# Decoder layer on one core: projected keys leave PSUM once as f32, and GpSimd makes both of their f16 parts

## What is computed

```python
q = _qdq(x) @ _qdq(wq).T + bq                  # x: the normed output of self-attention
kv = cond @ wkv.T + bkv                        # cond = ctx_2048: (16, 1500, 256) -> 512 columns
k, v = jnp.split(kv, 2, axis=-1)
q, k, v = ...                                  # 16 heads of 16
scores = jnp.einsum('bhnd,bhmd->bhnm', q, k) * Dh ** (-0.5)
out = softmax(scores) @ v
```

## Time and profile before

| what | us |
|---|---|
| median of 3 runs | 855.14 |
| lowest and highest run | 854.62, 862.06 |
| the profiled execution | 854.35 |
| its span, first to last instruction | 852.5 |

### The profile page before, as it was taken

How to read it: one execution, slowest core, us unless ns; L and a number is a source line. 1 busy time by engine, 2 the same in 40 slices (tenths; PEclk the granted TensorE clock), 3 DMA queues, 4 the chain that set the end, 5 groups by cost and what they waited for, 6 DMA issues and landing times.

```text
span 852.5 us, 30042 instructions
## 1 busy us (share of the span) xinstructions
PE 774.4 (91%) x12379; PEld 582.8 (68%) x12379; DVE 638.2 (75%) x1234; ACT 511.5 (60%) x1084; POOL 296.9 (35%) x366
## 2 busy tenths in 40 slices
PE   5689989999998999999999999999898899999996
PEld 3366666576666666666666666666665579999995
DVE  5877777868877878785977778786875745688887
ACT  2347656566565657655665666666665543787772
POOL 3263216223712371254126421732270003143232
PEclk9899999999999999999999999999999899999999
DMA  7356554554645546554655655565467976766643
GB/s 228 91 167 174 169 155 139 156 160 128 179 129 159 164 143 180 164 143 138 178 156 141 173 169 147 154 171 156 121 186 208 307 258 161 225 190 209 210 136 98
DMA packets 91380, 143.27 MB, mean 168 GB/s; under 512 B 11423, under 2 KB 79583, under 8 KB 87918
## 3 DMA queue, kind: packets, MB, share of 16 engines
q1 hardware_dynamic: 87742, 136.74, 53.6%
q0 software_dynamic: 3504, 4.62, 2.8%
HBM read 101.60 MB, written 39.68 MB: 166 GB/s over the span
## 4 chain that ended last, share of the span: by engine, by line
PE 57%; DVE 13%; DMA 11%; ACT 10%; issue 6%; SPq 1%; POOL 1%; DVEq 0%; POOLq 0%; ACTq 0%
PE ps L1659 15%; PE ps L1652 11%; DMA sums<-y_sb,g_token 10%; PE ps L1733 7%; PE ps L1711 6%; DVE negmax L522 4%; ACT pT L1441 3%; ACT k_front L1414 3%; PE ps L1971 3%; PE ps L1675 3%; DVE k_front L516 2%; PE ps L1992 2%; PE ps L1776 2%; PE ps L1620 2%; PE ps L1743 2%
## 5 line engine op out<-in xcount | busy, mean ns | idle before, releaser
L522 DVE TENSOR_REDUCE negmax<-ps 112x1 f32<-112x1500 f32 x121 | 207.4, 1714 | 32.1 <-PE ps L1675 31.9
L1441 ACT ACTIVATE pT<-ps 125x448 f32<-125x448 f32 x384 | 195.7, 546 | 21.9 <-PE ps L1711 18.2
L1265 POOL TENSOR_TENSOR ctx_lo<-ctx_raw,ctx_hi 128x250 f16<-128x250 f32 x188 | 119.3, 666 | 182.4 <-DVE ctx_hi L507 182.4
L1711 PE MATMUL ps<-qbd,k_st 97*128 97x112 f16 x1536 | 127.8, 214 | 17.3 <-ACT pT L1441 8.7
L1711 PEld LDWEIGHTS ps<-qbd,k_st 97*128 97x128 f16 x1536 | 91.2, 98 | 73.6 <-ACT pT L1441 20.1
L1397 ACT COPY v_sb<-ps 125x512 f32<-125x512 f32 x96 | 56.4, 587 | 83.5 <-PE ps L1659 83.4
L516 DVE SCALAR_TENSOR_TENSOR k_front<-ps,bk_sb,k_front 128x500 f16<-128x500 f32 x80 | 58.8, 735 | 63.0 <-ACT k_front L1414 63.0
L1733 PE MATMUL ps<-pT,v_sb 125*17 125x56 f32 x6144 | 92.1, 215 | 12.2 <-issue 12.2
L1733 PEld LDWEIGHTS ps<-pT,v_sb 125*17 125x17 f32 x6144 | 79.9, 98 | 31.9 <-issue 20.1
L1414 ACT ACTIVATE k_front<-ps,bk_sb 128x500 f16<-128x500 f32 x80 | 54.3, 678 | 62.3 <-PE ps L1652 62.3
L1659 PE MATMUL ps<-wkv_hi,ctx_hi 128*125 128x256 f16 x384 | 76.6, 281 | 10.5 <-DVE k_front L516 9.0
(11 more groups left out here) (263 smaller groups left out, 1492.7 us busy)
## 6 DMA issues: line engine op xcount, KB each, us to landing
k_st<-k_dram SPq DMA_DIRECT2D x288, 125.0 KB, 3.0
w_sb<-w SPq DMA_DIRECT2D x25, 1024.0 KB, 5.2
ctx_raw<-ctx_T SPq DMA_DIRECT2D x48, 500.0 KB, 3.7
k_dram<-k_front SPq DMA_DIRECT2D x80, 250.0 KB, 3.0
xs<-zeros SPq DMA_DIRECT2D x28, 260.0 KB, 4.4
w_sb<-w SPq DMA_DIRECT2D x8, 512.0 KB, 5.2
k_dram<-k_back SPq DMA_DIRECT2D x16, 250.0 KB, 2.9
xg<-xs SPq DMA_DIRECT2D x21, 130.0 KB, 4.1
```

The costliest lines, as they stand in the source:

```text
L522: V.tensor_reduce(negmax[0:QW], ps[0:QW, BANK_S:BANK_S + CHUNKS, 0:MC], AX.XY, ALU.max, negate=True).then_inc(max_done, 1)
L1265: last = nc.gpsimd.tensor_tensor(ctx_lo[:, k, c2, a], ctx_raw[:, k, c2, a], ctx_hi[:, k, c2, a], ALU.subtract)
L1441: nc.scalar.activation(pT[0:MT, (PAIRS * b + p) % 3, TPC * g:TPC * g + TPC], ps[0:MT, BANK_T + n % 2, 0:TPC * QW].rearrange("p (t n) -> p ...
L1711: last = mm(ps[:, BANK_T + n % 2, QW * i:QW * i + QW], k_st[:, j, p, a:a + P], qbd[:, j, p].rearrange("p h s -> p (h s)"), start=True, sto ...
```

## The change

ScalarE now writes a key unit as f32, bias added, into one of three buffers (`k_full`), and raises `unit_out` itself; VectorE no longer touches it. GpSimd gets a new step, `k_lo_step`, for each key unit of batches 1 to 15: two casts of 128x250 give the high f16 part, two subtractions of 128x250 the low one, into one of three buffers `k_two`. For batch 0 VectorE does the same from the f32 copy in two instructions of 500 columns. SP's `store_keys` waits for the new semaphore `k_lo_done`. Buffer waits: ScalarE waits for `k_lo_done` of the unit three before, GpSimd and VectorE for the DMA that stored it. PE's list stays as it was, ScalarE's too but for the name of what it writes.

```diff
 # ScalarE
+                n = key_number(b, u)
                 act.wait_ge(unit_done, UNITS * b + u + 1)
-                nc.scalar.activation(k_two[i][:, 0], ps[:, BANK_KV, 0:MC], ACT.Identity,
-                                     bias=bk_sb[:, g:g + 1]).then_inc(k_hi_done, 1)
+                if n >= 3:
+                    act.wait_ge(k_lo_done, n - 2)
+                nc.scalar.activation(k_full[n % 3], ps[:, BANK_KV, 0:MC], ACT.Identity, bias=bk_sb[:, g:g + 1]).then_inc(unit_out, 1)
 # VectorE, in the slots of every batch
-                    if units_on:
-                        for u in unit_slots(slot):
-                            unit_step(b + 1, 1 - j, u)
 # SP
-                sp.wait_ge(unit_out, UNITS * b + u + 1)
+                sp.wait_ge(k_lo_done, n + 1)
 # GpSimd
+            def k_lo_step(b, u):
+                n = key_number(b, u)
+                pool.wait_ge(unit_out, UNITS * b + u + 1)
...
+                pool.wait_ge(*stored(n - 3))
+                for half in range(2):
+                    a = slice(MC // 2 * half, MC // 2 * half + MC // 2)
+                    last = nc.gpsimd.tensor_copy(k_two[:, n % 3, 0, a], k_full[n % 3][:, a])
+                last.then_inc(k_hi_done, 1)
+                pool.wait_ge(k_hi_done, n + 1)
+                for half in range(2):
+                    a = slice(MC // 2 * half, MC // 2 * half + MC // 2)
+                    last = nc.gpsimd.tensor_tensor(k_two[:, n % 3, 1, a], k_full[n % 3][:, a], k_two[:, n % 3, 0, a], ALU.subtract)
+                last.then_inc(k_lo_done, 1)
+
             def iteration(it, t_before):
-                ctx_lo_step(2 * it + 1, 1, 1)
+                b = 2 * it + 1
+                ctx_lo_step(b, 1, 1)
+                k_lo_step(b, 0)
+                k_lo_step(b, 2)
                 if it > 1:
                     scatter(it - 2)
...
                 kbd_step(it + 1)
-                ctx_lo_step(2 * it + 1, 1, 2)
-                ctx_lo_step(2 * it + 2, 0, 0)
+                ctx_lo_step(b, 1, 2)
+                k_lo_step(b, 5)
+                k_lo_step(b, 6)
+                k_lo_step(b, 8)
+                ctx_lo_step(b + 1, 0, 0)
...
                 qbd_step(it + 1, 0, 1)
+                k_lo_step(b + 1, 11)
                 for h in range(2):
                     qbd_step(it + 1, 1, h)
```

More of the change, by code:

```diff
@@ L161, in decoder_layer @@
         wkv_lo = sb("wkv_lo", [P, CH, 2 * D], F16)
-        k_front = sb("k_front", [P, 5, 2, MC], F16)
+        k_two = sb("k_two", [P, 3, 2, MC], F16)
+        k_full01 = sb("k_full01", [P, 2, MC])
         sb("behind_k_front", [P, 8], F32)
@@ L168, in decoder_layer @@
         k_st = sb("k_st", [KA, 2, PAIRS, M + 4], F16)
-        k_back = sb("k_back", [P, 2, MC], F16)
+        k_full2 = sb("k_full2", [P, MC])
         sb("behind_keys", [P, 616])
@@ L220, in decoder_layer @@
         b_oqT = a_t2[:, D:D + P].bitcast(BF16).rearrange("p (c n) -> p c n", c=CH)
-        k_two = [k_front[:, n] for n in range(5)] + [k_back]
+        k_full = [k_full01[:, 0], k_full01[:, 1], k_full2]
         staging = pT[:].rearrange("p a m n -> p (a m n)")
@@ L273, in decoder_layer @@
         k_hi_done = sem("k_hi_done")
+        k_lo_done = sem("k_lo_done")
         unit_out = sem("unit_out")
@@ L434, in key_place, with key_number, stored @@
             return CH * c + g
-        def stored(b, u):
-            n = KEY_UNITS.index(u)
-            return k_out[n % 2], 16 * (len(KEY_UNITS) // 2 * b + n // 2 + 1)
+        def key_number(b, u):
+            return len(KEY_UNITS) * b + KEY_UNITS.index(u)
+        def stored(n):
+            return k_out[n % 2], 16 * (n // 2 + 1)
         def loaded(b):
@@ L511, in unit_step @@
                 if g in KEYS:
[L512 to L517, removed]
+                    n = key_number(b, u)
+                    dve.wait_ge(unit_out, UNITS * b + u + 1)
+                    if n >= 3:
+                        dve.wait_ge(*stored(n - 3))
+                    V.tensor_copy(k_two[:, n % 3, 0], k_full[n % 3]).then_inc(k_hi_done, 1)
+                    dve.wait_ge(k_hi_done, n + 1)
+                    V.tensor_tensor(k_two[:, n % 3, 1], k_full[n % 3], k_two[:, n % 3, 0], ALU.subtract).then_inc(k_lo_done, 1)
             def max_step(b, p):
@@ L1082, in store_keys @@
                 c, g = UNIT[u]
-                i = key_place(c, g)
-                sp.wait_ge(unit_out, UNITS * b + u + 1)
+                i, n = key_place(c, g), key_number(b, u)
+                sp.wait_ge(k_lo_done, n + 1)
                 if not (isinstance(b, int) and b == 0):
                     sp.wait_ge(k_in[g], loaded(b - 1))
-                sp.dma_start(k_dram[i], k_two[i]).then_inc(stored(b, u)[0], 16)
+                sp.dma_start(k_dram[i], k_two[:, n % 3]).then_inc(stored(n)[0], 16)
                 for dst, src in between:
@@ L1094, in load_keys @@
                 i = key_place(c, g)
-                sp.wait_ge(*stored(b, u))
+                sp.wait_ge(*stored(key_number(b, u)))
                 for r, part in enumerate(KEY_PARTS[c]):
@@ L1293, in qbd_step @@
                     pool.wait_ge(st_done, CHUNKS * PAIRS * (2 * t + j - 1))
-                if j == 1:
+                if j == 1 and (h == 1 or t == 0):
                     pool.wait_ge(qbd_done, 8 * t + 4 + 2 * h)
+                elif j == 1:
+                    pool.wait_ge(k_lo_done, 2 * len(KEY_UNITS) * t + len(KEY_UNITS))
+                elif h == 0 and not first:
+                    pool.wait_ge(k_lo_done, 2 * len(KEY_UNITS) * t + len(KEY_UNITS) - 1)
                 elif first and h == 0:
@@ L1334, in iteration @@
                 kbd_step(it + 1)
-                ctx_lo_step(2 * it + 1, 1, 2)
-                ctx_lo_step(2 * it + 2, 0, 0)
+                ctx_lo_step(b, 1, 2)
[3 more added lines that the diff above has]
+                ctx_lo_step(b + 1, 0, 0)
                 if t_before is not None:
                     b_rstd_step(t_before)
-                ctx_lo_step(2 * it + 2, 0, 1)
+                k_lo_step(b, 11)
+                ctx_lo_step(b + 1, 0, 1)
+                k_lo_step(b + 1, 0)
+                k_lo_step(b + 1, 2)
                 rstd_step(it + 1)
-                ctx_lo_step(2 * it + 2, 0, 2)
+                ctx_lo_step(b + 1, 0, 2)
+                k_lo_step(b + 1, 5)
+                k_lo_step(b + 1, 6)
+                k_lo_step(b + 1, 8)
                 qbd_step(it + 1, 0, 0)
-                ctx_lo_step(2 * it + 3, 1, 0)
+                ctx_lo_step(b + 2, 1, 0)
                 qbd_step(it + 1, 0, 1)
+                k_lo_step(b + 1, 11)
                 for h in range(2):
@@ L1373, in _ @@
             ctx_lo_step(B - 1, 1, 1)
+            k_lo_step(B - 1, 0)
+            k_lo_step(B - 1, 2)
             scatter(TILES - 3)
             ctx_lo_step(B - 1, 1, 2)
+            k_lo_step(B - 1, 5)
             b_rstd_step(TILES - 2)
+            for u in (6, 8, 11):
+                k_lo_step(B - 1, u)
             scatter(TILES - 2)
```

2 lines of the change are left out of this document (added).

## The result

The changed kernel takes **877.42 us** (median of 4 runs, 876.45 to 881.18); the kernel before took 854.88 beside it (4 runs, 848.51 to 862.06). The ratio is **1.0298, 95% interval 1.0257 to 1.0339**: slower by 22.5 us. The forecast was 863, range 847 to 879. So the direction was right, and the time lies at the upper end of the range, 14 us above the forecast; the loss is nearly three times the 8.0 us of the forecast's sum. The profiled execution took 876.49 (span 874.7), 22.1 more than that of before. The ratios go by the fast runs alone and the medians by all runs, so the two need not agree to the last digit. TensorE's granted clock differs a little from run to run of one kernel (0.979 to 0.993 over 30 runs of the kernel before) and the time with it, so a profiled execution can lie some us off the median of its kernel.

A forecast was written before the change was run, and what follows sets the result against it. PE was taken as the bound, held by VectorE's read-outs. Four scatter pairs +9.2, the fifth -0.4, first two pairs -0.8, start -1.0, last pair +1.0 sum to +8.0 us, giving 863 on the medians' scale, range 847 to 879.

The forecast's parts named there:

- The forecast's own case: Key steps on POOL make the self-attention products late and PE stands: 857 to 871 us, chance 0.44.
- Rival 4: VectorE and POOL hold each other up throughout: key step 3.0 us, +21 us, 876; chance 0.13.
- Rival 5: PE's stalls bring TensorE's clock down, 12.8 us on top of 863 in five pairs: 876; chance 0.11.
- PE waits for keys in flight at head pairs 0 or 4: Sign that the forecast is wrong: PE waiting at those head pairs for keys still being loaded.
- The removal: VectorE's key read-outs go: PE's waits of 9.0 + 2.0 us and 1.1 for the row of maxima, 12.1 at most.
- The key step: On POOL, two casts and two subtractions of 250 columns plus semaphore waits: 2.2 us, bounds 1.8 and 2.8.
- Products 2.4 us late in five pairs, 2.9 with a meeting: Three POOL steps ahead delay PE's self-attention 2.4 us per scatter pair; a VectorE-POOL meeting adds 0.5; 0.59 won elsewhere.
- five times and 2 to 3 us each: Sign that the forecast is right: PE's waits for `a_kbd`, the self-attention products, in the profile after.
- The first two pairs: No scatter, products in time; unit 11's load, behind unit 0's store, eats 0.66 won: -0.4 a pair, -0.8 us.
- The last pair: Scatter and context step in POOL's chain but no products; unit 6 some 1 us later: +1.0 us.
- the gain of the start: PE's 2.0 us read-out wait goes, VectorE's two instructions cost some 0.3 more six times: -1.0, between -2.5 and +1.8.
- Rivals 1 and 2: First: POOL keeps up and PE wins, 843 or 847, chance 0.18. Second: gain and loss cancel, 855, chance 0.14.

The follow-up runs named there:

- the empty steps: Kernel before plus three unneeded GpSimd steps of key-step shape, ahead of the self-attention products (`a_kbd`): 871.94 us; the same placed behind them: 852.61 us.
- the load first: Changed kernel with SP issuing the load of unit 11 ahead of the store of unit 0, likewise in the last block: 867.29 us.

## Why the prediction was right and wrong

The forecast's own case ran from 857 to 871. That 877.42 still lies within 847 to 879 is owed to the room given to rivals 4 and 5, and one of its own signs of being wrong came true: "PE waits for keys in flight at head pairs 0 or 4".

- **The removal** (12.1 us at most). Right in the main: the read-out waits are gone, and alone that is worth 7.9. The 1.1 for `nm_row` did not go; VectorE still held PE there for 1.7 us in the changed kernel.
- **The key step** (2.2 us, bounds 1.8 and 2.8). Right: 2.14 busy. Cast and subtraction were worked out as 0.41 and 0.62; medians 0.39 and 0.66 in the empty steps.
- **Products 2.4 us late in five pairs, 2.9 with a meeting.** Right in size: 2.5 to 2.7 alone in four of the five, 16.1 / 5 = 3.2 with the load first. In the changed kernel part of it shows as a wait for keys, so the forecast's waits for `a_kbd`, "five times and 2 to 3 us each", were not what the profile showed; the five pairs came to 5.9 us, forecast 8.8.
- **The first two pairs**: this is the term that failed. The forecast said that the load of unit 11 lands at "some 312.9, against 312.74", that it "eats the 0.66", and that "-0.4 a pair is left". The second pair cost +6.1. From the end of the second query step on (297.42 there, 136.39 in the changed kernel), the forecast had unit 0's key step done after 11.2 us and the load landed after 15.5. Measured: 11.5 (147.87) and 17.8 (154.21). Of the 2.3 us between them 0.3 is POOL, 0.4 the issue of the store, which was not counted, 0.1 the issue of the load, and 1.5 the flight: 154.21 - 149.69 = 4.5 us after the last issue, where the median of 3.0 was taken. In the eight pairs this flight went from 2.2 to 4.5. The 2.3, the 0.66 that PE had won and the 0.16 by which the forecast had the load late make 3.1 of PE's wait of 3.24. To that came the clock, 0.94 in this pair: PE's busy time grew by 3.7.
- **The last pair** ("its unit 6 comes some 1 us later"). It cost 9.8. The same load is late there by 4.80 us, which the forecast, having found the case in the first two pairs, did not carry over; PE's busy time grew by 3.75 there too. A piece of the experts' `w2` is issued between the store and the load in this pair. Unit 6 was not the wait; with the load first it is, for 0.9 us. The first pair lost 2.9 us at the load as well and came out at +0.7, with the gain of the start set against it. The run with the load first confirms both terms: 78.96 and 67.60 us in their place.
- **Rival 5, the clock.** The sum had nothing for it; in the profiled executions it took 9.8 of the 22.1 us. It was not an alternative to the waits but came with them. Within one kernel time follows the clock: 30 runs of the kernel before, at 0.979 to 0.993, lie about a line of 6.8 us for each 0.01. The changed kernel ran at 0.969 to 0.972. The line carried on beyond its points to 0.970 gives 866, so by this estimate half of the 22.5 us is clock. That the waits bring it down is shown by the empty steps: the same work ran at 0.979 to 0.988 ahead of `a_kbd`, with the waits, and at 0.985 to 0.993 behind it, without. Not every wait does so: behind 323.86, a wait of 2.54, the clock stayed at 1.00, behind 489.26, a wait of 2.53, it was 0.57 for 4 us. What decides that, these runs don't show. The Trainium skill (TensorE: Matmul & The Clock Gate, section "HAM oscillation — how this bites in real kernels") describes waits for DMA after which a kernel's matmuls run cold; the stretches behind 154.21, 240.82 and 654.66 (clock 0.50, 0.61 and 0.56) agree with it, that behind 72.18, after a wait of 2.93, doesn't (1.00).
- **Rivals 1 and 2** needed a step of 1.4 and 1.8 us: no. **Rival 4** needed 3.0: no. Single meetings, as the port rule of the Trainium skill (SBUF — State Buffer, "Who interferes with whom") has them, are in the way to 147.87: query products of 1.20 and 1.25 us instead of 0.93, beside a rotary step and a cast on VectorE.
- **Fewer buffers**, three for the finished keys instead of six, were no cause in the changed kernel: all idle time of the casts there is put down to `k_full`, all of ScalarE's copy to PE.

Not tried: the last pair by itself, with the w2 pieces moved.

## What to carry to other kernels

When a step moves to another engine, follow its product through every list that waits for it to the engine that is the bound: here a DMA list in order turned a late store into a late load of something else. A slack of a few tenths of a microsecond, worked out with a median flight, is to be priced as a stall, in every stage where the same place occurs, the last one too. And move the steps behind which nothing urgent is queued: half the work moved won 6.7 us, all of it lost 22.5.

## What the runs showed of the hardware

- A GpSimd cast of 128x250 from f32 to f16 takes 0.39 us, a two-input subtraction of the same size 0.66; no cast of this size was in the trace before.
- A 250 KB store issued 0.5 us behind a 500 KB load took 7 us until the load that waits for it could be issued, against a median of 3.0 to landing; three loads of 125 KB were issued in between. With the context load moved away (239.36 to 244.61) it was 5.25.
- Five PE waits of 0.8 to 2.7 us, 11.1 in all, cost 18 us in time; 7.0 of it is PE's own work at a lower clock. In two of the five pairs the clock stayed at 1.00, in the others it was 0.96 to 0.98.
- Behind waits of 2.1 to 4.8 us TensorE's granted clock was at its lower level in some cases (0.50 in the 4 us behind a wait of 3.24) and not in others (1.00 behind one of 2.93).
